# One-hot matrices of the second stage: whole pieces on ScalarE, split pieces by one compare per chunk

## The reference, cut to what matters

```python
def _spmm_plus_eye(rows, cols, vals, X):
    msgs = vals[:, None] * X[cols]
    agg = jax.ops.segment_sum(msgs, rows, num_segments=N)
    return agg + X

support = feature @ W1                                  # feature: layer norm of x
out = _spmm_plus_eye(src, dst, edge_weight, support)    # first sum over edges
out = _batchnorm_relu(out, gamma, beta)
out = _spmm_plus_eye(src, dst, edge_weight, out @ W2)   # second sum over edges
x = x + out
x = x + moe(layernorm(x))                               # 8 experts, top 2
```

## Time and profile before

| | us |
|---|---|
| median of three runs | 4682.11 |
| the profiled execution, its own time | 4687.35 |
| its span in the trace | 4685.5 |
| second stage, 1260 to 2110 us | 850 |
| of it busy: TensorE / VectorE / GpSimd / ScalarE | 724.55 / 717.63 / 626.22 / 361.91 |

### The profile page before, as it was taken

One profiled execution on the slowest core, in us unless ns is written; L12 is line 12 of the kernel. 1 busy time (PEld: TensorE's weight loads), 2 busy tenths in 40 slices (PEclk: granted clock), 3 DMA queues, 4 the chain that ended last, 5 costly groups with the idle time before them and its releaser, 6 DMA issues.

```text
span 4685.5 us, 86280 instructions
## 1 busy us (share of the span) xinstructions
PE 3908.0 (83%) x28087; PEld 3406.3 (73%) x28087; DVE 3591.2 (77%) x7898; ACT 2982.4 (64%) x6052; POOL 3237.6 (69%) x3177
## 2 busy tenths in 40 slices
PE   1688888888788888885688988888888988888898
PEld 1688888888677767673467777777777777777788
DVE  8788888999688888885557677777777777767776
ACT  3799888999744444444356666666666666656665
POOL 0466666677677777673777777777777777777762
PEclk6799999999899999996579999999999999999999
DMA  7788888988798888876433434343433434343331
GB/s 234 275 317 324 318 320 323 332 313 296 283 308 298 296 307 309 296 267 172 130 103 115 121 113 116 113 121 113 116 113 113 122 113 116 113 120 113 113 97 45
DMA packets 323796, 928.69 MB, mean 198 GB/s; under 512 B 50896, under 2 KB 132896, under 8 KB 320848
## 3 DMA queue, kind: packets, MB, share of 16 engines
q0 software_dynamic: 153216, 483.15, 31.1%
q1 hardware_dynamic: 167960, 426.60, 28.1%
q10 hardware_dynamic: 2172, 13.35, 0.8%
HBM read 597.06 MB, written 325.83 MB: 197 GB/s over the span
## 4 chain that ended last, share of the span: by engine, by line
PE 32%; DMA 18%; POOL 14%; DVE 14%; issue 11%; ACT 10%; SPq 1%; DVEq 0%; ACTq 0%; POOLq 0%
POOL X L1258 9%; DMA X<-h,tabT 7%; PE ps L1407 6%; DMA msgd<-A,tabT 6%; PE ps L1428 5%; DMA L<-msgd 4%; PE ps L1297 3%; ACT A L867 3%; PE ps L1204 2%; POOL mL L1157 2%; PE ps L802 2%; PE ps L771 2%; PE ps L1301 2%; PE ps L1012 2%; PE ps L803 2%
## 5 line engine op out<-in xcount | busy, mean ns | idle before, releaser
L1258 POOL DMA_INDIRECT X<-h,tabT x1620 | 1667.8, 1030 | 588.5 <-issue 383.7
L1286 ACT ACTIVATE gH<-X,tabT 128x256 fp32r<-128x256 f32 x1080 | 531.8, 503 | 518.6 <-DMA X<-h,tabT 502.5
L916 POOL DMA_INDIRECT msgd<-A,tabT x464 | 568.5, 1225 | 332.0 <-ACT A L867 207.3
L867 ACT ACTIVATE A<-ps,A 128x256 f32<-128x256 f32 x1856 | 745.8, 519 | 76.4 <-PE ps L803 73.4
L1275 DVE SCALAR_TENSOR_TENSOR gL<-X,tabT,gH 128x256 fp32r<-128x256 f32 x1080 | 505.9, 480 | 300.6 <-ACT gH L1286 278.5
L802 PE MATMUL ps<-winH,DT 128*128 128x256 f32 x1856 | 510.5, 307 | 50.8 <-issue 36.1
L1299 PE MATMUL ps<-gH,s 128*125 128x256 f32 x1200 | 397.6, 332 | 182.7 <-DVE s L1268 95.9
L1140 ACT ACTIVATE mH<-L 128x1280 fp32r<-128x1280 f32 (+1 forms) x267 | 307.7, 1165 | 377.5 <-DMA L<-msgd 346.9
L1157 POOL TENSOR_TENSOR mL<-L,mH 128x256 fp32r<-128x256 f32 x267 | 384.2, 1439 | 150.6 <-ACT mH L1140 90.9
L803 PE MATMUL ps<-winL,DT 128*128 128x256 f32 x1856 | 471.3, 286 | 0.0
L1299 PEld LDWEIGHTS ps<-gH,s 128*125 128x125 f32 x1200 | 240.2, 200 | 273.9 <-issue 138.0
(11 more groups left out here) (267 smaller groups left out, 10703.1 us busy)
## 6 DMA issues: line engine op xcount, KB each, us to landing
L<-msgd SPq DMA_DIRECT2D x200, 650.0 KB, 6.0
L<-msgd SPq DMA_DIRECT2D x200, 520.0 KB, 5.9
A<-sbd SPq DMA_DIRECT2D x58, 805.0 KB, 6.4
msgd<-A SPq DMA_DIRECT2D x100, 390.0 KB
X<-h,tabT POOLq DMA_INDIRECT x1620, 2.8
winR<-h SPq DMA_DIRECT2D x116, 128.0 KB
A<-in_x SPq DMA_DIRECT2D x10, 1120.0 KB
h<-A ACTq DMA_DIRECT2D x10, 1120.0 KB
```

The source lines that it names most:

```text
L867: e.activation(M[:, n, 0:F], psum[4 + v % 4][:, (n % 2) * F:(n % 2 + 1) * F], ACT.Identity, scale=M[:, n, F + 2:F + 3]).then_inc(evc, 1)
L916: e.indirect_dma_start(msgd, bass.IndirectOffsetOnAxis(ap=idxI[g % 4][:, t:t + 1], axis=0), msg[g % 3][:, t * 4 * RW:(t + 1) * 4 * RW], No ...
L1258: e.indirect_dma_start(B.G[c % GRL], None, h2, bass.IndirectOffsetOnAxis(ap=tab3[:, c, 0:1].bitcast(I32), axis=0)).then_inc(gatl[c % GRL], 16)
L1286: e.activation(B.gH[c % HR2][:, :], B.G[c % GRL], ACT.Identity, scale=w_).then_inc(g_hi, 1)
```

## The change: what it does

For whole pieces `S` moves from VectorE to ScalarE. ScalarE computes per chunk the square of (row number - column) (`Square` with scale -1 and the row number as a per-partition bias), 4 or 5 instructions of 128x125; it waits on its own semaphore `r_sq`, then one `Relu` over the whole piece gives 1 - square where that is positive, which is 1 at equality and 0 elsewhere, in place. It waits for the load and for the ring slot of `S` (piece u-4 multiplied) before the squares.

For split pieces VectorE still makes `S`, but with one `tensor_scalar` compare of 128x125 per chunk (4 or 5 a piece) in place of one `tensor_tensor` over the piece. Its input is not `iota_f` but a copy with gaps: 25 groups of 5 numbers at a pitch of 6. Two small instructions make the copy and a column of ones at the stage's start. Readers of `S` and GpSimd's copy wait on `r_sel` for split pieces and on the new `r_sela` for whole ones (`selected`). VectorE's `parts` returns at once for whole pieces.

```diff
+IOW = 6
 class Read:
+                self.gap = st("gap", R // 5 * IOW + 1)
+                self.iota = self.gap[:, 0:R // 5 * IOW].rearrange("p (a b) -> p a b", b=IOW)[:, :, 0:5]
+                self.one = self.gap[:, R // 5 * IOW:R // 5 * IOW + 1]
+        def selected(e, u):
+            v = split_upto(u, whole)
+            if whole(u):
+                e.wait_ge(r_sela, u + 1 - v)
+            else:
+                e.wait_ge(r_sel, v)
 def act_read(e, B):
             def high(u):
                 n, L3, H, Lo, S3 = B.of(u)
+                e.wait_ge(ldm[u % LR], 16 * (u // LR + 1))
                 if whole(u):
+                    if u >= SRD:
+                        e.wait_ge(r_mm, u - SRD + 1)
+                    if u == 1:
+                        e.wait_ge(r_sel, 1)
+                    for k in range(n):
+                        e.activation(S3[:, k, :], iota_f[:, 0:R], ACT.Square, bias=L3[:, k, F + 1:F + 2], scale=-1.0).then_inc(r_sq, 1)
+                    e.wait_ge(r_sq, sum(PIECES[x][2] for x in range(u + 1) if whole(x)))
+                    e.activation(S3, S3.bitcast(F32), ACT.Relu, bias=B.one, scale=-1.0).then_inc(r_sela, 1)
                     return
-                e.wait_ge(ldm[u % LR], 16 * (u // LR + 1))
 def pool_read(e, B), and pe_read(e, B) likewise:
-                e.wait_ge(r_sel, u + 1)
+                selected(e, u)
-        def dve_read(e, B):
+        def dve_read(e, B, own):
+            own.done(e.tensor_copy(B.iota, iota_f[:, 0:R].rearrange("p (a b) -> p a b", b=5)))
+            own.done(e.memset(B.one, 1.0))
+            e.wait_ge(own.s, own.n)
             def parts(u):
                 n, L3, H, Lo, S3 = B.of(u)
+                if whole(u):
+                    return
                 e.wait_ge(ldm[u % LR], 16 * (u // LR + 1))
                 if u >= SRD:
                     e.wait_ge(r_mm, u - SRD + 1)
-                e.tensor_tensor(S3, iota_f[:, 0:R].rearrange("p (o f) -> p o f", o=1).broadcast_to([P, n, R]),
-                                L3[:, :, F + 1:F + 2].broadcast_to([P, n, R]), ALU.is_equal).then_inc(r_sel, 1)
-                if not whole(u):
-                    e.wait_ge(r_hi, split_upto(u, whole))
-                    terms_free(e, u, r_mm)
-                    e.tensor_tensor(Lo[:, 1:n, :], ...).then_inc(r_lo, 1)
+                for k in range(n):
+                    m = e.tensor_scalar(S3[:, k, :].rearrange("p (a b) -> p a b", b=5), B.iota, L3[:, k, F + 1:F + 2], None, ALU.is_equal)
+                m.then_inc(r_sel, 1)
+                e.wait_ge(r_hi, split_upto(u, whole))
+                terms_free(e, u, r_mm)
+                e.tensor_tensor(Lo[:, 1:n, :], ...).then_inc(r_lo, 1)
```

More of the change, by code:

```diff
@@ L352, in build @@
         ldm = [sem_1(f"ldm{k}") for k in range(LR)]
-        r_hi, r_sel, r_lo, r_lop, r_tab, r_mm, r_add = (sem_1(n) for n in ("r_hi", "r_sel", "r_lo", "r_lop", "r_tab", "r_mm", "r_add"))
+        r_hi, r_sel, r_sq, r_sela, r_lo, r_lop, r_tab, r_mm, r_add = (sem_1(n) for n in ("r_hi", "r_sel", "r_sq", "r_sela", "r_lo", "r_lop", "r_tab", "r_mm", "r_add"))
         g_sel, g_hi, g_lo, g_mm, g_add = (sem_1(n) for n in ("g_sel", "g_hi", "g_lo", "g_mm", "g_add"))
@@ L1166, in parts @@
                     e.wait_ge(r_mm, u - SRD + 1)
-                e.tensor_tensor(S3, iota_f[:, 0:R].rearrange("p (o f) -> p o f", o=1).broadcast_to([P, n, R]),
-                                L3[:, :, F + 1:F + 2].broadcast_to([P, n, R]), ALU.is_equal).then_inc(r_sel, 1)
-                if not whole(u):
-                    e.wait_ge(r_hi, split_upto(u, whole))
-                    terms_free(e, u, r_mm)
-                    e.tensor_tensor(Lo[:, 1:n, :], L3[:, 1:n, 0:F], H[:, 1:n, :].bitcast(F32), ALU.subtract).then_inc(r_lo, 1)
+                for k in range(n):
[3 more added lines that the diff above has]
+                terms_free(e, u, r_mm)
+                e.tensor_tensor(Lo[:, 1:n, :], L3[:, 1:n, 0:F], H[:, 1:n, :].bitcast(F32), ALU.subtract).then_inc(r_lo, 1)
             parts(0)
@@ L2090, in ordered @@
                 own = Own(own_f)
-                dve_read(e, RB)
+                dve_read(e, RB, own)
                 dve_bn(e, own)
```

## The result

The change gains nothing. In the first measurement the kernel with the change took 4690.99 us against 4684.24 us (medians of 20 runs each), a ratio of 1.0019 (95% interval 1.001 to 1.0027). Measured again beside the last experiments it was 0.9999 (0.9985 to 1.0012). The prediction was 4627 us, 55 us less than the kernel before.

A forecast was written before the change was run, and what follows sets the result against it. VectorE was taken to bound the 850 us stage. Afterwards VectorE's floor of 783 us and ScalarE's 782, plus 12 us, gave 795, 55 less, so 4627 us; forecast's own range 4600 to 4660, wide range 4587 to 4700.

The forecast's parts named there:

- VectorE paces the stage: Second stage: VectorE sets the pace of its 850 us, with the DMA engines only 14% behind.
- 718 + 134 = 852: VectorE in the second stage: 718 us busy plus 134 us of waits (dense1 copies, loads, `mH`) make the whole stage.
- DMA 0.86 x 850 = 731 us: Floor of the second stage from the loads: the DMA engines' share of 0.86 times its 850 us.
- What goes and comes on VectorE: VectorE's one-hot compares: 339 us go, 312 us of small ones at 0.26 us come, -27 us (-111 to +46).
- the relief of `mL`: VectorE's `mL` no longer slowed by GpSimd's reads: 42 us taken as gone, bound 0.
- ScalarE +290 us: ScalarE's squares and `Relu` for 133 whole pieces at 2.18 us each: 290 us, bounds 221 and 350.
- The load waits of ScalarE as cover: ScalarE's 347 us of waiting for loads hides its new work; these waits fall to under 60 us.
- the first rival: ScalarE's in-order list paces the stage, slower once over 78 us of load waits remain; 4714 us; chance 0.20.
- Another sign of being wrong: TensorE's waits move from `mL` to ScalarE's `S` or `mH`; no size given.
- The gaps: Rival: small compares run two elements a cycle despite the table's gaps, `mL` and GpSimd stay slowed; 4622 us; chance 0.06.
- VectorE is not relieved: Rival: compares at 0.32 us, VectorE at 856 us with `mL` relieved; about 4685 us; chance 0.12.
- the wide range: Whole kernel time: from 4587 us, where all comes apart well, up to 4700, inside ScalarE pacing the stage.

The follow-up runs named there:

- light_before: Kernel before the change, second-stage loads cut to 3 of a piece's 4 or 5 chunks from the seventh piece on; 4656.77 us, ratio 0.9943, loop 802.8 us.
- act_only: Kernel with the change, but split pieces again get one two-input compare per piece, leaving only the move of whole pieces to ScalarE; ratio 1.0028, loop 843.6 us.
- behind_cut_after: behind_after with only one square per whole piece in place of 4 or 5 from the fifth piece on; ratio 1.0083, loop 741.8 us.
- behind_before: Kernel before the change with all of dense1 moved behind the last piece; ratio 1.0138, loop 747.1 us.
- behind_after: Kernel with the change and all of dense1 moved behind the last piece; ratio 1.0149, loop 761.2 us.
- nogap: Kernel with the change, split pieces' compares reading the plain table of 125 numbers in place of the one with gaps; ratio 1.0055, loop 847.1 us.
- spread kernel: Kernel before the change with each dense1's three steps taken one after each of three pieces; 4642.11 us, ratio 0.993, loop 784.7 us.

## Why the prediction was wrong, point by point

- *VectorE paces the stage, "with the DMA engines only 14% behind it".* This is the step that failed: the order was the other way round. light_before shows VectorE's floor at 803 us for a loop of 828, so VectorE was 25 us behind the loads. The sum 718 + 134 = 852 was true of the trace, but 46 us of its 134 were waits for loads and `mH`, in which the true bound showed. And SyncE's 396 us of waits for slots were read as the lateness of VectorE; with 56 us less work on VectorE they did not shrink (476 us; for all engines together 650 against 666).
- *"DMA 0.86 x 850 = 731 us" as a floor.* The same step in the sum. About 115 us of idle DMA time stayed when VectorE got faster; some 76 of them arise while TensorE is in dense1 and releases no slot. That 731 and 115 add up to the stage is no evidence, since they must; the evidence is that the loop falls to 803 us with the loads cut, to 785 with dense1 spread and to 747 with dense1 out of it, and that VectorE's relief shows (31 us) only with the loads cut. So the floor of the loads in the stage as it was built is the 828 us of the loop, or nearly, and not 731.
- *What goes and comes on VectorE.* 0.26 us a compare: in order of time five take 1.34 us, (1.34 - 0.33) / 4 = 0.25. Right. -69 us in all was said, -56 measured; the relief of `mL` is 27 us (121 x 134 + 81 x 133 ns), not 42. This was mis-sized, but it decides nothing.
- *ScalarE +290 us.* The groups are busy for 187.6 + 54.1 + 47.8 = 289.5 us, and the whole engine for 264 us more than before. Right as a size. Its price was seen in the wrong place: the prediction asked whether ScalarE has the time, and not how much later each whole piece is released. act_only (ratio 1.0028) shows that there is a price, and behind_cut_after that it goes with the squares; the 14 us between the loops of behind_before and behind_after are its size only as far as two single profiles can tell.
- *The load waits of ScalarE as cover.* 133 us remained where under 60 were said, above the 78 from which the first rival was to decide. But the stage got no longer by it: the waits were not on top of ScalarE's work, they were the loads' own pace. Another sign of being wrong that was named came true too: TensorE's weight loads wait 32.5 us and its products 25.4 us for ScalarE's one-hots. And the DMA share, which was to rise above 0.9, stayed at 0.86.
- *The rivals.* The gaps work. That VectorE is not relieved, the case nearest to the right time (4685; by its own stage of 856 us it should have been 4688), had the wrong mechanism: it was relieved, by 56 us, and nothing came of it. The case that happened, a resource with share 0.86 that is the bound, was not among them. That the measured 4691 us lies inside the wide range (4587 to 4700) is luck: the range reaches there only for ScalarE pacing the stage.

## What to carry to other kernels

Before a mean share of 0.86 is taken for 14% of room, cut it into stretches shorter than one round of the loop: full, empty, full is a bound with holes. Here the order of the consumer that holds the slots narrowed them. Then check a bound from both sides by making the other one light: had the loads been cut first, 803 against 828 us would have shown that VectorE is not what holds the loop, and 772 what its relief is worth once the loads are out of the way. And moving work to an engine with idle time is not free where a slot waits for that work.

## What the runs showed of the hardware that I had not expected

- Small compares that read the table with gaps run at 321 to 348 ns beside GpSimd. Reading the plain table, the same instruction has a median of 275 and a maximum of 858 ns (nogap), and its mean (367) is above the slower form's 332.
- The burst that loads `acc` (1 KB rows) keeps the DMA engines at a share of 1.08 to 1.19 with only 210 to 256 GB/s, in twelve stretches of 4 us of the kernel before; in the 68 other stretches that are full (0.97 to 1.03) they move 368 GB/s on average. Loading it block by block goes with a loop 24 us shorter than that of the spread kernel (784.7 to 761.1), each from one profile and on different chips. Why it helps is not shown.
